# One ring of two PSUM banks for maxima, projections and turned outputs, in both attentions of a four-stage layer stack

## The reference, cut to what matters

```python
x = x + _layernorm(_L0_attn_ref(_layernorm(x), ...))   # 16 heads of 8, two rounds of attention
x = x + _layernorm(_L0_ffn_ref(_layernorm(x), ...))    # 8 experts, top 2, and a shared one
x = x + _layernorm(_L1_attn_ref(_layernorm(x), ...))   # global and windowed attention, summed
x = x + _layernorm(_L1_ffn_ref(_layernorm(x), ...))    # 16 gated experts, top 2, and a shared one
```

```python
state = q
for _ in range(STEPS):          # STEPS = 2
    sim = jnp.einsum('bqhd,bkhd->bqhk', state, k)
    att = jax.nn.softmax(BETA * sim, axis=-1)
    state = jnp.einsum('bqhk,bkhd->bqhd', att, v)
o = state.reshape(B, S, H) @ Wo + bo
```

## Time and profile before

| | |
|---|---|
| median of three runs | 1807.33 us (1806.85 to 1808.82) |
| profiled execution, its own time | 1805.99 us |
| its span | 1804.2 us |
| TensorE busy | 1519.9 us, 84% |
| VectorE busy | 1197.0 us, 66% |
| ScalarE busy | 1019.0 us, 56% |
| GpSimd busy | 784.9 us, 44% |
| mean granted clock of TensorE | 0.946 of full speed |
| first attention, about | 80 to 600 us of the span |
| second attention, about | 920 to 1560 us of the span |

### The profile page before, as it was taken

The page is one execution under the profiler, slowest core; times in us unless marked ns, Lnnn a source line. Parts: engine busy times, 40 slices in busy tenths (PEclk is TensorE's granted clock), DMA queues, the critical chain, the costliest instruction groups (busy, mean ns, idle before and its releaser), DMA issues. The chain is left out here.

```text
span 1804.2 us, 37712 instructions
## 1 busy us (share of the span) xinstructions
PE 1519.9 (84%) x12057; PEld 1150.1 (64%) x12057; DVE 1197.0 (66%) x3314; ACT 1019.0 (56%) x1870; POOL 784.9 (44%) x1008
## 2 busy tenths in 40 slices
PE   2599999989999587998169989888988999589997
PEld 1366767667666466987046656666656666378886
DVE  2367777767766456997556766676767766556676
ACT  1388787777776255776026555555555666434332
POOL 7755564674652344996653334333333221101111
PEclk9899999999999699999569999999999999889999
DMA  5000000010010110222111111111111111000000
GB/s 189 19 19 19 17 19 19 23 31 20 25 36 15 33 56 24 72 71 58 67 39 35 36 39 29 30 34 31 31 31 32 30 31 31 4 1 6 12 10 20
DMA packets 75098, 60.50 MB, mean 34 GB/s; under 512 B 17088, under 2 KB 71104, under 8 KB 74560
## 3 DMA queue, kind: packets, MB, share of 16 engines
q1 hardware_dynamic: 70848, 50.21, 9.7%
q0 software_dynamic: 4096, 8.40, 1.6%
HBM read 20.01 MB, written 13.37 MB: 19 GB/s over the span
## 5 line engine op out<-in xcount | busy, mean ns | idle before, releaser
L1261 DVE TENSOR_REDUCE a_qt<-a_ps_m 128x2 fp32r<-128x512 f32 (+1 forms) x384 | 264.8, 690 | 161.9 <-PE a_ps_m L1047 113.6
L524 ACT ACTIVATE a_p<-a_ps_s 128x1024 f32<-128x1024 f32 x256 | 264.0, 1032 | 33.9 <-PE a_ps_s L385 27.3
L633 DVE TENSOR_REDUCE a_qt<-a_ps_m 128x2 fp32r<-128x512 f32 x256 | 176.6, 690 | 87.8 <-PE a_ps_m L396 85.4
L791 POOL TENSOR_TENSOR a_rn<-a_ss,a_half 128x16 f32<-128x16 f32 x64 | 186.2, 2916 | 1.4
L1047 PE MATMUL a_ps_m<-a_kpad,a_qs 128*128 128x512 f32 x256 | 130.3, 509 | 55.1 <-DVE a_qt L1261 50.9
L1174 ACT ACTIVATE a_pg<-a_ps_s 128x1024 f32<-128x1024 f32 x128 | 131.7, 1030 | 17.0 <-PE a_ps_s L1022 12.1
L403 PE MATMUL a_ps_o<-a_p,a_v 128*32 128x256 f32 x2048 | 137.1, 385 | 3.0 <-ACT a_p L524 1.6
L396 PE MATMUL a_ps_m<-a_kpad,a_qs 128*128 128x512 f32 x256 | 116.9, 457 | 15.3 <-DVE a_qt L633 13.3
L1047 PEld LDWEIGHTS a_ps_m<-a_kpad,a_qs 128*128 128x128 f32 x256 | 50.0, 195 | 104.8 <-DVE a_qt L1261 85.0
L1013 PE MATMUL a_ps_a<-ident,a_qt 128*128 128x128 f32 x512 | 109.6, 297 | 5.4 <-ACT a_qsm L1168 3.8
L1492 POOL COPY a_v<-a_vt 128x64 f32<-128x64 f32 x64 | 15.3, 239 | 223.4 <-PE a_ps_o L1124 223.3
(11 more groups left out here) (362 smaller groups left out, 4334.4 us busy)
## 6 DMA issues: line engine op xcount, KB each, us to landing
a_kpad<-a_ks SPq DMA_DIRECT2D x768, 32.0 KB, 1.9
f_xin<-xs SPq DMA_DIRECT2D x39, 128.0 KB, 2.1
ys<-f_yout SPq DMA_DIRECT2D x39, 128.0 KB, 2.1
w<-in_w SPq DMA_DIRECT2D x2, 2304.0 KB, 11.2
out_x<-X SPq DMA_DIRECT2D x8, 256.0 KB, 2.3
xs<-f_zero SPq DMA_DIRECT2D x15, 128.0 KB
wgu<-in_wgu SPq DMA_DIRECT2D x1, 1152.0 KB, 5.2
xs<-Z,r_at POOLq DMA_INDIRECT x64
```

The lines of the kernel that those rows point to most:

```text
L524: nc.scalar.activation(probs[:, u % 2, 2 * c:2 * c + 2, :, :].rearrange("p a b c -> p (a b c)"), ps_s[:, n % 2, :], ACT.Exp).then_inc(exp_ ...
L633: nc.vector.tensor_reduce(qt2[:, k % 2, 2 * part:2 * part + 2, SHIFT], ps_m[:, :, :], AX.X, ALU.max, negate=True).then_inc(max_done, 1)
L791: nc.gpsimd.tensor_tensor(rn[:, part * c:(part + 1) * c], ss[:, part * c:(part + 1) * c], half[:, 0:c], ALU.pow).then_inc(rn_ready, 1)
L1261: nc.vector.tensor_reduce(dst, src, AX.X, ALU.max, negate=True).then_inc(max_done, 1)
```

## The change

In each attention `ps_m` and `ps_b` become two banks `ps_d`, which all maxima, projections, turned outputs and output products use in turn. `D_ORDER` is the order of the tasks within a step, and `d_count` numbers them through the whole stage. `bank` takes the bank by that number's parity. The two pairs of semaphores become one pair, `d_full` and `d_done`. Before TensorE writes a task's bank it waits until VectorE has finished the task two places before it (`d_count - 2`). For this, TensorE and VectorE must take the tasks in the same order, so two things move: in the first attention VectorE reads op after it has reduced m2 instead of before, and in the second TensorE issues m0, with the waits for the padded K and for Q that stand before it, ahead of the projections wq and q instead of behind them.

The core of the diff; what is left out replaces `b_count`, `b_done`, `max_done` and `ps_b` by `d_count`, `d_done`, `d_done` and the task's bank in the same way, in waits of VectorE and GpSimd too:

```diff
@@ -199,7 +199,7 @@
     FIRST, LAST = -3 * NG, UNITS + 3 * NG - 1
 
     A_ORDER = ("T1", "T2", "K", "xT", "yT", "zT", "Q")
-    B_ORDER = ("qp", "lg", "place", "kp", "vp", "O2", "op", "O1")
+    D_ORDER = ("qp", "m0", "lg", "place", "kp", "vp", "m1", "O2", "m2", "op", "O1", "m3")
 
...
@@ -268,18 +268,16 @@
         o2 = sb("o2", [P, S])
 
         ps_s = pb("ps_s", [P, 2, 1024])
-        ps_m = pb("ps_m", [P, 2, S])
         ps_o = pb("ps_o", [P, 512])[:, 0:S]
         ps_a = pb("ps_a", [P, 512])[:, 0:S]
-        ps_b = pb("ps_b", [P, 512])[:, 0:S]
+        ps_d = [pb(f"ps_d{n}", [P, 512]) for n in range(2)]
 
         tiles_ready = sem("tiles_ready")
         scores_full, exp_done = sem("scores_full"), sem("exp_done")
         o1_full, o1_copied = sem("o1_full"), sem("o1_copied")
         o2_full, o2_copied = sem("o2_full"), sem("o2_copied")
-        max_full, max_done = sem("max_full"), sem("max_done")
         a_full, a_done = sem("a_full"), sem("a_done")
-        b_full, b_done = sem("b_full"), sem("b_done")
+        d_full, d_done = sem("d_full"), sem("d_done")
         qt2_ready = sem("qt2_ready")
...
@@ -304,10 +302,12 @@
                     "yT": r == 1 and batch(b - 2), "xT": r == 2 and batch(b + 3),
                     "zT": r == 3 and 0 <= b - 3 < ROUTED}[task]
 
-        def b_live(k, task):
+        def d_live(k, task):
 
             b, r = k // NG, k % NG
             projects = r == 3 and batch(b + 3)
+            if task in ("m0", "m1", "m2", "m3"):
+                return unit(k - 2)
             return {"qp": projects, "kp": projects, "vp": projects, "O2": unit(k - 4),
...
             return a_table[k, task]
 
-        def b_count(k, task):
-            return b_table[k, task]
+        def d_count(k, task):
+            return d_table[k, task]
+
+        def bank(k, task):
+            return ps_d[(d_count(k, task) - 1) % 2]
+
+        def narrow(k, task):
+            return bank(k, task)[:, 0:S]
 
         def chunks(k, which):
 
...
             pe.wait_ge(a["loaded"], 16 * a["loads"])
 
-            def wait_b(st, task):
-                wait(pe, b_done, st.at(lambda k: b_count(k, task) - 1))
+            def wait_d(st, task):
+
+                wait(pe, d_done, st.at(lambda k: d_count(k, task) - 2))
 
...
                 u, t, c = st.k - 2, part // 2, part % 2
 
-                wait(pe, max_done, st.at(lambda k: 4 * clip(k - 2, UNITS) + part))
-                nc.tensor.matmul(ps_m[:, :, :].rearrange("p a b -> p (a b)"), qs2[:, u % 2, t * P:(t + 1) * P],
+                wait_d(st, f"m{part}")
+                nc.tensor.matmul(bank(st.k, f"m{part}")[:, :], qs2[:, u % 2, t * P:(t + 1) * P],
                                  kpad[:, u % RING, 2 * c:2 * c + 2, :].rearrange("p a b -> p (a b)"),
-                                 start=True, stop=True).then_inc(max_full, 1)
+                                 start=True, stop=True).then_inc(d_full, 1)
 
             def attend(u, probs, full):
                 for t in range(TPB):
...
 
             def project(st, n, task):
-                wait_b(st, task)
+                wait_d(st, task)
                 for t in range(TPB):
-                    last = nc.tensor.matmul(ps_b[:, t * P:(t + 1) * P], xT[:, t * P:(t + 1) * P],
+                    last = nc.tensor.matmul(narrow(st.k, task)[:, t * P:(t + 1) * P], xT[:, t * P:(t + 1) * P],
                                             a["wqkv"][:, n * D:(n + 1) * D], start=True, stop=True)
-                last.then_inc(b_full, 1)
+                last.then_inc(d_full, 1)
 
             for st in steps(pe):
...
                 if r == 2 and batch(b - 2):
                     pe.wait_ge(a_done, st.at(lambda k: a_count(k - 1, "yT")))
-                    wait_b(st, "op")
+                    wait_d(st, "op")
                     for t in range(TPB):
-                        last = nc.tensor.matmul(ps_b[:, t * P:(t + 1) * P], yT[:, t * P:(t + 1) * P],
+                        last = nc.tensor.matmul(narrow(k, "op")[:, t * P:(t + 1) * P], yT[:, t * P:(t + 1) * P],
                                                 a["wo"][:, :], start=True, stop=True)
-                    last.then_inc(b_full, 1)
+                    last.then_inc(d_full, 1)
                 if unit(k + NG):
                     nb, g = (k + NG) // NG, r
                     pe.wait_ge(stacks_ready, st.at(lambda k: 2 * ((k + NG) // NG + 1)))
                     wait_a(st, "Q")
                     transposes(ps_a, lambda t: stacked(qt[:, nb % 2, t * H + g * G:t * H + (g + 1) * G, :]), a_full)
                 if unit(k - 1):
-                    wait_b(st, "O1")
+                    wait_d(st, "O1")
                     pe.wait_ge(o1_copied, st.at(lambda k: k))
-                    transposes(ps_b, lambda t: o1[:, t * P:(t + 1) * P], b_full)
+                    transposes(narrow(k, "O1"), lambda t: o1[:, t * P:(t + 1) * P], d_full)
                 if unit(k - 3):
                     score_chunk(st, 3, qs2m[:, :])
                 maxima(st, 3)
...
                     if not unit(k - 2):
                         return
-                    dve.wait_ge(max_full, st.at(lambda k: 4 * clip(k - 2, UNITS) + part + 1))
-                    nc.vector.tensor_reduce(qt2[:, k % 2, 2 * part:2 * part + 2, SHIFT], ps_m[:, :, :], AX.X, ALU.max,
-                                            negate=True).then_inc(max_done, 1)
+                    dve.wait_ge(d_full, d_count(k, f"m{part}"))
+                    nc.vector.tensor_reduce(qt2[:, k % 2, 2 * part:2 * part + 2, SHIFT],
+                                            bank(k, f"m{part}")[:, :].rearrange("p (a b) -> p a b", b=S), AX.X,
+                                            ALU.max, negate=True).then_inc(d_done, 1)
 
...
                         src[:, :, 0:HD].rearrange("p (t h) d -> p t h d", t=TPB),
                         r2[:, :].rearrange("p (t h) -> p t h", t=TPB).unsqueeze(3).to_broadcast([P, TPB, G, HD]),
-                        ALU.mult).then_inc(b_done, 1)
-                if r == 2 and batch(b - 2):
-
-                    dve.wait_ge(b_full, st.at(lambda k: b_count(k, "op")))
-                    dve.wait_ge(zb_ready, st.at(lambda k: k // NG - 1))
-                    nc.vector.tensor_tensor(y[:].rearrange("p t d -> p (t d)"), ps_b, Z[:, tiles(st, -2)],
-                                            ALU.add).then_inc(b_done, 1)
+                        ALU.mult).then_inc(d_done, 1)
                 if r == 1 and batch(b - 3):
                     moments(st, "new", 0, mv_b).then_inc(stats_b, 1)
                 if r == 0 and batch(b + 3):
                     moments(st, "x", TPB, mv_a).then_inc(stats_a, 1)
                 maxima(2)
+                if r == 2 and batch(b - 2):
+
+                    dve.wait_ge(d_full, st.at(lambda k: d_count(k, "op")))
+                    dve.wait_ge(zb_ready, st.at(lambda k: k // NG - 1))
+                    nc.vector.tensor_tensor(y[:].rearrange("p t d -> p (t d)"), narrow(k, "op"), Z[:, tiles(st, -2)],
+                                            ALU.add).then_inc(d_done, 1)
                 if unit(k - 1):
 
-                    dve.wait_ge(b_full, st.at(lambda k: b_count(k, "O1")))
-                    src = heads_out(ps_b)
...
-    B_ORDER = ("wq", "q", "v", "wk", "k", "Og", "Ow", "op")
+    D_ORDER = ("m0", "wq", "q", "v", "m1", "wk", "m2", "k", "m3", "Og", "m4", "Ow", "m5", "op")
 
     def steps(eng):
         for k in range(FIRST, LOOP[0] * ROUND):
...
                     return n
 
-        def b_count(k, task):
-
-
-            n = (2 * clip(k - 2, UNITS) + 2 * before(k - 2, 2) + 2 * before(k - 3, 2) + before(k, 1)
-                 + before(k - 3, -1))
+        def d_count(k, task):
+
+            n = (6 * clip(k, UNITS) + 2 * clip(k - 2, UNITS) + 2 * before(k - 2, 2) + 2 * before(k - 3, 2)
+                 + before(k, 1) + before(k - 3, -1))
             b, r = k // NG, k % NG
             live = {"wq": r == 2 and batch(b + 2), "wk": r == 2 and batch(b + 2), "q": r == 3 and batch(b + 2),
                     "k": r == 3 and batch(b + 2), "v": r == 0 and batch(b + 1), "Og": unit(k - 2),
                     "Ow": unit(k - 2), "op": r == 3 and batch(b - 1)}
-            for name in B_ORDER:
-                n += live[name]
+            for name in D_ORDER:
+                n += live.get(name, unit(k))
                 if name == task:
                     return n
 
+        def bank(k, task):
+            return ps_d[(d_count(k, task) - 1) % 2]
+
+        def narrow(k, task):
+            return bank(k, task)[:, 0:S]
+
         def chunk(k, which):
 
             return 3 * clip(k - 1, UNITS) + which + 1
-
-        def maxes(k, part):
-            return 6 * clip(k, UNITS) + part + 1
 
         @block.sync
...
                     return
                 u = st.k
-                wait(pe, max_done, st.at(lambda k: maxes(k, part) - 1))
+                wait_d(st, f"m{part}")
+                dst = bank(st.k, f"m{part}")
```

(22 more changed lines are left out.)

137 lines of the change are left out of this document (70 added, 67 removed).

## The result

The changed kernel takes 1775.51 us (median of four runs, 1775.32 to 1776.81), and the kernel before took 1808.07 us beside it. The ratio is 0.9821 (0.9805 to 0.9837): 32.6 us faster, where 16 were forecast. The time lies outside the forecast's range. Three later sets of the same kernel gave 0.9818 (e5), 0.983 (e9) and 0.9823 (e13). The profiled execution took 1775.4 us, 30.6 less than that of before.

The account below looks back on a forecast made before the run. Each attention was taken to last as long as TensorE's work plus its idle time before matmuls. 17.8 us won less 2.8 lost made net 15.0, so 1791.0 profiled and 1792 us forecast, range 1785 to 1799 (8 in 10: 1781 to 1802).

Parts of the forecast that it names:

- Two others, at either end of the stage, had 0.36 and 0.57 us: 0.9 us: Second attention: idle time before two further m1, outside the ten of r=1, ends, winning 0.9 us.
- r=1, ten times 0.95 us, and r=3, 0.20 lost each: Second attention: r=1 wins 9.5 us before m1 and attend; q waiting behind m0 in r=3 loses 2.8 over fourteen batches.
- O1 in r=2: First attention: O1 waits for m2's reduction instead of y, winning 0.34 us in 11 undisturbed batches, 3.7 us.
- The first unit: First attention: m1 is issued before m0's reduction ends and m2 waits for it instead, winning 1.6 us.
- The three late m1: First attention, r=2: m1 held 1.8 us by GpSimd's powers; 0.4 us each plus one clock fall gone, 2.1 us.
- falls from 50.9 to about 40: Second attention: TensorE's wait in us for VectorE's reduction before maxima matmuls, the rest all in r=0 and r=2.
- (b): First attention, m1 in r=2: mostly nothing won; in three late cases O2 then stops at m0's reduction; sum 2.1 us.
- no change: Rival: waits the order keeps set the pace, r=2 gives back r=1's gain; 1804 to 1810 us, chance 0.11.
- the gain is handed on: Rival: TensorE stops a little later at ScalarE's copies instead; 1799 to 1803 us, chance 0.14.
- slower: Rival: second attention's Og waits for m2's late reduction, 64 times; 1811 us at 0.3 us late, chance 0.06.
- All waits end: Rival: all 68.0 us of TensorE's waits in both attentions go, giving 1739 us; chance 0.01.
- The rival about the clock: Rival: half a clock fall costs 1.4 us, one more in each of 14 batches 20 us, 1812; chance 0.02.

Follow-up runs that it names:

- e5: The changed kernel unaltered, measured again to compare other runs with: 1773.60 us, ratio 0.9818 to the kernel before.
- e9: The changed kernel unaltered, measured again in another set: 1780.56 us, ratio 0.983 to the kernel before.
- e13: The changed kernel unaltered, measured again in the last set: 1780.24 us, ratio 0.9823 to the kernel before.
- e8: Changed kernel, but from step 48 of the second attention each task also waits for the last of its own kind: 1784.34 us, ratio 0.9864.
- e14: The same kernel as e8, run once more beside e13: 1785.72 us, ratio 0.986 to the kernel before.
- e6: Changed kernel with old same-kind waits only in steps before any maximum runs (first attention k under 2, second under 0): 1781.96 us, ratio 0.9859.
- e7: Changed kernel with old same-kind waits only in steps 0 to 3 of the second attention: 1781.24 us, ratio 0.9857.
- e4: Changed kernel with old same-kind waits at the ends (first attention k below 6; second below 4 and from 48): 1788.15 us, ratio 0.9937.
- e2: First attention of the kernel before with the changed second attention: 1783.69 us, ratio 0.9912 to the kernel before.
- e3: Changed kernel with two banks and new order, but every task also waits for the last of its own kind: 1808.15 us, ratio 1.0047.

## Why the forecast was wrong, step by step

The sign was right, the reading of the order was right for the steady step, and the time was missed by 15.6 us of the profiled 30.6. The step that failed is the one put as "Two others, at either end of the stage, had 0.36 and 0.57 us: 0.9 us". It looked at the ends with the eyes of the steady step, for m1 in r=1, and did not go through the order again with the tasks that live there. In steps 0 and 1 there are no outputs yet and nothing is attended, so from m1 of step 0 to m5 of step 1 the ring holds maxima alone. In step 0 m2 to m5 each waited for the reduction before (0.36, 0.79, 0.36 and 0.36 us), in step 1 m1 (0.36, the only one of them that the forecast counted). In the opening, projections stand in a row in the same way. The tasks between which the steady step alternates are simply not there, and it was their alternation that made most waits stay. The rows for this were in the trace of before. The openings and steps 0 to 3 make 1.5 + 3.3 + 5.6 = 10.4 us of the miss.

- *r=1, ten times 0.95 us, and r=3, 0.20 lost each:* right. From trace to trace the distance from m5 to m1 is 0.95 to 0.98 shorter in r=1, and 0.20 to 0.22 longer in r=3. The ten m1, from 988.05 to 1354.35 in the profile after, lie 366.30 us apart, nine batches of 40.70; 40.7 was forecast. q waits 0.25 us, as said. In r=2 the change is 0.00, as costed, as long as VectorE mixes there.
- *Steps 4 to 63 of the second attention:* from m1 of step 4 to m0 of step 48 (447.28 us before, 440.18 after) 7.1 us were won against 9.5 - 11 x 0.20 = 7.3: right. Steps 48 to 63 won 2.1 (141.53, then 139.43) against 0.57 - 2 x 0.20 = 0.2: m1 of step 49 gave 0.7, and steps 62 and 63 gave 2.0, where m0 no longer waits for m5, which the low end of the range had and the sum had not; the swap cost 0.35 in r=3 and another 0.42 in the two steps with r=2 (50 and 54) that have no long wait to hide it. In e8 and e14 the old waits cost 3.6 us there.
- *Opening and steps 0 to 3 of the second attention:* 0 and 0.2 us were forecast, 3.3 and 5.8 measured (e6: 3.2; e7: 3.9; e4 beside e2: 3.5 and 6.9). Of the 5.8, 2.6 us are waits of maxima for reductions that ended (3.1 before step 4, 0.5 after), and 0.7 of that came back as other idle time. The other 3.9 are matmuls that took less time, with a clock that rises 10 us earlier.
- *Before the first attention:* 1.5 us, again projections in a row (e6: 2.4); not forecast.
- *First attention, O1 in r=2:* 0.34 forecast, 0.35 to 0.36 in most batches: right. The first unit: 1.6 forecast, 2.3 measured, the mechanism as said (m2 starts 7.02 us after the first m0; it was m1 that started 7.73 after it, and these 0.7 us were not forecast). The three late m1: 2.1 forecast, 1.5 + 0.5 + 0.5 measured; one of two clock falls went in this profile, both in e5's (granted clock 1.00 in all three places), where it is 3.7. The forecast's one was picked between none and two, and e9 and e13 have one as well. O2 stops at the same reduction, as said (3.1 us in three), but for up to 1.5 us and not at most 1.2. Another 0.5 came at m3 of the last unit.
- *Signs:* "falls from 50.9 to about 40" was wrong, 28.3. The difference is 8.6 us in r=1 before m1, 5.6 in r=1 before m0 (handed on to ScalarE's copy, whose wait before L1024 is 12.7 in place of 3.8), 2.3 in r=2, and 1.9 and 4.3 in steps 0 to 3 and from 48. All that is left does lie in r=0 and r=2, as said. No wait arose before Og, the clock of the second attention is 0.98, and r=2's wait fell from 1.16 to 0.94. New waits before O2 did arise, three of them; the prediction names them both as expected, under (b), and as a sign of being wrong, so this sign says nothing.

Of the rivals, *no change*, *the gain is handed on* and *slower* did not come. *All waits end* did not either: 28.3 us stayed, 17.5 in r=0 and 10.7 in r=2. The 0.06 "if the same waits were worth more than their idle time says" named the direction and no mechanism, and its 1778 to 1785 us did not reach far enough. The rival about the clock had only the bad side; what the clock gives back where idle time goes was asked for the three late m1 alone (0.9 us), not for the opening.

On that point the Trainium skill was read too narrowly. "TensorE: Matmul & The Clock Gate", section "A second HAM failure mode: psum-queue depth-cycling", ties clock falls to short idle times between groups of matmuls. The mean clock of a whole attention, 0.97, was set against it, and a mean over 640 us does not show a fall of 7 (5.3 to 12.1 us after the first maximum in e7). The traces of e7 and e3 agree with it in steps 0 to 3, where the granted clock goes from 1.00 to 0.50. Here cycling through two banks was the remedy (e2 and e8 stay at 1.00), since the idle times came from using one.

Open: why the times of e6, e7 and e8 lie 3 to 7 us further above e5 than their edited steps. Windows of unchanged code differ by as much between runs of one kernel (the expert stage between the attentions took 236.9, 238.0, 240.8 and 244.1 us in four profiles of the changed kernel), so part of it is chance. That it all is was not shown. The same stage was 1.8 us shorter in the profile after than in that of before; this part of the miss stays open too.

## What to carry to other kernels

When a buffer rule looks n tasks back, go through the order of tasks once for the steady step and once for each filling and draining step, with only the tasks that live there; the second attention got 3.3 + 5.1 = 8.4 of its 17.6 us in its opening and its first four of 64 steps. A bank more ends waits only where the task before last is done, so what an engine queues ahead of its answer is a separate question, and it was worth 10.6 us without any ring. Work moved out of one engine's late place needs a place where it is free: the mixing had one; for the head of r=0 the one place that was tried had none.

## What the runs showed of the hardware

One and the same kernel comes into the second attention at either clock level (e8 at 1.00, e14 at 0.50), which makes 1.2 us in steps 0 to 3 (31.0 and 32.2). What a stretch with idle time does to the clock is the larger effect. With one maximum at a time it fell from 1.00 to 0.50 in e7 (TensorE busy for 2.53 and 2.85 of 4 us before and while it fell) and in e3 (2.53 and 2.77), and stayed at 0.50 for 15 us in before and e4 (in the first three windows of 4 us busy for 3.64, 2.50 and 3.19). With the ring it stayed at 1.00 in e2 and e8 (3.46 and 2.98), and where it came in at 0.50 it was back at 1.00 after 4 to 5 us (after, e5, e9, e13, e14). Maxima matmuls that take 0.48 to 0.50 us at the higher level take 0.77 to 0.80 at the lower. So a wait of 0.36 us there can cost more than 0.36 us: steps 0 to 3 lost 1.9 us of idle time and, with it, 3.9 us of busy time. In e7 the old waits put back 2.7 us of idle time and 1.2 of busy time beside e5, although it came in at the higher level and e5 at the lower.
